# Attention and mixture-of-experts block: the eight attention heads that carry two chunks of expert weights moved from the 41st to 48th to the 49th to 56th

## What is computed

```python
h = _layernorm(x, axis=-1) * (1 + ca) + sa
x = x + ga * _L0_attn_ref(h, wq, wkv_a, wkv_b, wo)      # 16 heads, causal, latent k/v of 128, rope of 64
h = _layernorm(x, axis=-1) * (1 + cb) + sb
x = x + gb * _L0_ffn_ref(h, wa, rg, rgb, rw1, rb1, rw2, rb2, sg, sgb, sw1, sb1, sw2, sb2)
```

## Time and profile before

| | us |
|---|---|
| median of 3 runs | 1380.09 |
| the runs | 1380.09, 1387.56, 1379.63 |
| the profiled execution | 1384.28 |
| its span, first to last instruction | 1382.4 |

### The profile page before, as it was taken

One profiled execution on the slowest core, in us unless ns is written; L12 is line 12 of the kernel. 1 busy time (PEld: TensorE's weight loads), 2 busy tenths in 40 slices (PEclk: granted clock), 3 DMA queues, 4 the chain that ended last, 5 costly groups with the idle time before them and its releaser, 6 DMA issues. The chain is left out here.

```text
span 1382.4 us, 22778 instructions
## 1 busy us (share of the span) xinstructions
PE 1342.6 (97%) x6900; PEld 1113.9 (81%) x6900; DVE 854.7 (62%) x1753; ACT 672.2 (49%) x1551; POOL 385.0 (28%) x352
## 2 busy tenths in 40 slices
PE   6999999999999999999998999998999999999997
PEld 3667777888888888888887888887787888888885
DVE  5788745666666666666775666665766443434567
ACT  3334326666666666666665666664422332323222
POOL 0335465000012091030550120910023323223163
PEclk9999999999999999999999999999999999999999
DMA  9999989967677669696799866693827888887475
GB/s 293 369 345 373 367 299 310 338 216 226 202 275 265 227 227 321 200 336 203 241 362 330 303 204 231 219 362 128 324 101 273 304 323 333 314 333 265 129 226 171
DMA packets 160057, 375.57 MB, mean 272 GB/s; under 512 B 23164, under 2 KB 80576, under 8 KB 147696
## 3 DMA queue, kind: packets, MB, share of 16 engines
q1 hardware_dynamic: 144416, 314.32, 65.0%
q0 software_dynamic: 15568, 60.32, 12.4%
HBM read 245.84 MB, written 128.22 MB: 271 GB/s over the span
## 5 line engine op out<-in xcount | busy, mean ns | idle before, releaser
L1183 ACT ACTIVATE a_pr<-a_pr,a_stat 128x128 f32<-128x128 f32 (+3 forms) x256 | 142.3, 557 | 112.0 <-DVE a_stat L1258 111.7
L1258 DVE CUSTOM_DVE_ANT_0 a_pr<-a_psS,f_mask 128x128 f32<-128x128 f32 (+3 forms) x256 | 116.6, 486 | 33.1 <-PE a_psS L1366 30.7
L1189 ACT ACTIVATE a_pr<-a_pr,a_stat 128x128 f32<-128x128 f32 (+3 forms) x256 | 122.1, 549 | 0.5 <-DVE a_stat L1263 0.5
L1378 PE MATMUL a_psY<-a_pT,a_cv 128*128 128x512 f32 x564 | 120.5, 357 | 0.3 <-issue 0.3
L1378 PEld LDWEIGHTS a_psY<-a_pT,a_cv 128*128 128x128 f32 x564 | 101.4, 188 | 23.3 <-issue 0.7
L1202 ACT ACTIVATE a_pT<-a_psT 128x512 fp32r<-128x512 f32 x128 | 69.4, 597 | 79.0 <-PE a_psT L1394 79.0
L102 PE MATMUL a_psX<-a_hT,a_wqk 128*128 128x512 f32 (+1 forms) x256 | 101.3, 396 | 4.9 <-DVE a_pT L1286 4.3
L104 PE MATMUL a_psX<-a_hT,a_wqk 128*128 128x512 f32 (+1 forms) x256 | 101.6, 397 | 0.0
L103 PE MATMUL a_psX<-a_hT,a_wqk 128*128 128x512 f32 (+1 forms) x256 | 101.3, 396 | 0.0
L1274 DVE SCALAR_TENSOR_TENSOR a_qT<-a_psX,a_qT 128x512 fp32r<-128x512 f32 x64 | 44.3, 691 | 85.1 <-ACT a_qT L1193 85.1
L1286 DVE TENSOR_TENSOR a_pT<-a_psT,a_pT 128x512 fp32r<-128x512 f32 x128 | 82.1, 682 | 12.3 <-ACT a_pT L1202 12.3
(11 more groups left out here) (375 smaller groups left out, 3566.0 us busy)
## 6 DMA issues: line engine op xcount, KB each, us to landing
w1s_d<-a_ws SPq DMA_DIRECT2D x72, 512.0 KB, 3.6
a_wqk<-wqk_d SPq DMA_DIRECT2D x64, 512.0 KB, 4.6
a_mh<-mhl_d SPq DMA_DIRECT2D x32, 1024.0 KB, 5.9
s_ring<-w1s_d SPq DMA_DIRECT2D x16, 2048.0 KB, 9.3
w2s_d<-a_ws SPq DMA_DIRECT2D x72, 256.0 KB, 4.0
qpe_d<-p_qs SPq DMA_DIRECT2D x16, 1024.0 KB, 5.0
a_rw<-in_L_ffn_rw SPq DMA_DIRECT2D x128, 128.0 KB, 3.5
a_qpe<-qpe_d SPq DMA_DIRECT2D x64, 256.0 KB, 2.7
```

The costliest lines, as they stand in the source:

```text
L1183: nc.scalar.activation(pr[i], pr[i], ACT.Exp, bias=nmax[:, i:i + 1], scale=-1.0, accum_out=rsum[:, i:i + 1]).then_inc(ex, 1)
L1189: nc.scalar.activation(pr[i], pr[i], ACT.Copy, scale=rinv[:, i:i + 1]).then_inc(nr, 1)
L1258: nc.vector.tensor_tensor_reduce(out=pr[i], in0=score[i][:, 0:w], in1=mask[:, S - w:S], scale=-1.0, scalar=3e38, op0=ALU.add, op1=ALU.min, ...
L1378: last = nc.tensor.matmul(two_of(bank)[:, :, (2 - k) * P:2 * P], cv[:, j, cs], pT[:, :, ps, o:o + k * P], start=m == 0, stop=m == len(part ...
```

## The change

`DBL` goes from (10, 12) to (12, 14), so that the doubled heads are g = 48 to 55 and `EARLY` is 48. The phases move with it. In g = 40 to 47 the chunks of the routed experts come one a head, and the chunks of the shared experts are split eight heads later. The waits and the reads back of the shared experts' weights before the last group follow `EARLY`. The group left behind the doubled ones (m = 14) is written out in place of a loop over m = 12 to 14 on PE, ScalarE and SyncE, and over m = 14 alone on VectorE; VectorE gets a loop over m = 10 and 11. The groups m = 12 and 13 on VectorE now have both a second chunk and, in m = 13, the statistics of the norm.

```diff
--- before.py
+++ after.py
@@ -983,7 +983,7 @@
         ends = [psS[:, 2], psZ[:, :]]
         rest = [(B * PAIRS - 2, 3)] + [(B * PAIRS - 1, t) for t in range(TB)]
         two_of = lambda bank: bank.rearrange("p (u n) -> p u n", u=2)
-        DBL = (10, 12)
+        DBL = (12, 14)
         EARLY = DBL[0] * 4
 
         def run(eng, pair, norms=False):
@@ -1001,7 +1001,7 @@
                     two(m, 0)
                 for m in range(*DBL):
                     two(m, 1)
-                with eng.Fori(DBL[1], B * QB - 1) as m:
+                for m in range(DBL[1], B * QB - 1):
                     two(m, 2)
             else:
                 with eng.Fori(2, QB) as m:
@@ -1012,11 +1012,12 @@
                     two(m, 0)
                 two(2 * QB, 0)
                 two(2 * QB + 1, 0, 1)
-                for m in range(*DBL):
-                    two(m, 1)
-                two(3 * QB, 2)
-                two(3 * QB + 1, 2, 2)
-                with eng.Fori(3 * QB + 2, B * QB - 1) as m:
+                with eng.Fori(2 * QB + 2, DBL[0]) as m:
+                    two(m, 0)
+                assert DBL == (3 * QB, 3 * QB + 2)
+                two(DBL[0], 1)
+                two(DBL[0] + 1, 1, 2)
+                for m in range(DBL[1], B * QB - 1):
                     two(m, 2)
             pair(B * PAIRS - 2, 0, 4, False, 2, None)
             pair(B * PAIRS - 1, 1, 4, True, 2, None)
@@ -1103,7 +1104,7 @@
                 four(DBL[0] - 1, 4, 0)
                 for m in range(*DBL):
                     four(m, 4, 1)
-                with sp.Fori(DBL[1], B * H // 4 - 1) as m:
+                for m in range(DBL[1], B * H // 4 - 1):
                     four(m, 4, 2)
                 sp.wait_ge(ws_out[1], 32 * (EARLY // 2 + EXTRA + 1))
                 sp.dma_start(hT[:, 0].rearrange("p c s n -> p (c s n)").bitcast(F32),
```

## The result

| | before | changed |
|---|---|---|
| median of 20 runs each, us | 1380.95 | 1378.72 |
| lowest and highest | 1377.45, 1387.71 | 1375.42, 1382.33 |
| profiled execution, us | 1384.28 | 1378.67 |
| its span, us | 1382.4 | 1376.9 |

The ratio is 0.9973 with a 95% interval of 0.9962 to 0.9983: the kernel is 2.3 to 5.3 us faster. The prediction had 7.13 us, as a change of the median to 1373.0. The sign and the range of 1369 to 1381 held, the size did not.

What follows compares the result with a forecast made beforehand. TensorE, busy 97% of 1382.4 us, bounds the kernel, so only its idle or slow time can be gained. The stall's -7.13 us, all other terms 0, off the median 1380.09 gave 1372.96 us, range 1369 to 1381.

Steps and rivals of the forecast that it cites:

- The slack of 3.33 us: PE's spare time behind the late second chunk of g = 44: ScalarE waited 7.67 us, PE idled 4.34.
- the limit of 6.3 us between issue and landing: In doubled heads, a chunk landing more than 6.3 us after its issue costs PE time; a quiet pair needs 5.35 or less.
- nothing new would be lost: Eight chunks moved to g = 48 to 55 add no time on ScalarE, VectorE or DMA; at most 0.7 us if wrong.
- the 339 worked out for g = 48 and 49: GB/s of DMA traffic forecast for this first doubled pair: 7.87 MB in 23.2 us, including GpSimd's `a_cv`; cost 0.
- the 317: GB/s forecast for the three doubled pairs after g = 48 and 49, with no GpSimd transfer, like the pair at 750.
- The two terms put at 0 for the wait at g = 56 and for the loops: PE's wait of 0.42 us for `a_oT` at g = 56 stays; loops going or coming change nothing beyond 0.42 us.
- the bound of 0.42: Most that PE's wait at g = 56 could change, -0.42 to +0.42 us, also taken as the most for the loops.
- So the stall goes: -7.13 us: In heads 45 and 46, PE's 4.34 us of idle time and 2.79 of slow work disappear with single chunks.
- Rival 1: No gain, 1380.1 us: plain runs hardly have the stall, perhaps only the slowest and the profiled one; chance 0.17.
- Rivals 2 and 3: 2: small stall in g = 48 to 51, 1376 us, chance 0.09. 3: repeated stalls from g = 48, 1387.2 or 1394.4, 0.04.

## Why the prediction was right and wrong

- Where the stall is and whom it hits was right: the late chunk in `a_rw`, the slack of PE behind it, GpSimd's transfers as the cause. Moving GpSimd's 2 MB of loads alone left 0.61 us of it. The slack of 3.33 us, and the limit of 6.3 us between issue and landing built on it, hold only for a head's second chunk; behind a first chunk it is 1.1 to 1.3 us.
- That nothing new would be lost was right in every profile: g = 44 to 47, the doubled heads, and the heads with both a second chunk and the statistics. The pairs carry 290 and 332 GB/s for the 339 worked out for g = 48 and 49, and then 319 and 311 for the 317. Part of the first pair's traffic falls into the second.
- The two terms put at 0 for the wait at g = 56 and for the loops were not quite 0. The steps to g = 56 and 57, where VectorE's old loop began, are now 11.62 + 11.67 us for 12.07 + 11.79, 0.57 less and so beyond the bound of 0.42; those to g = 40 and 41, where its new loop begins, are 12.18 + 11.79 for 11.95 + 11.67, 0.35 more. The nine profiles with the old places and the ten with the new ones repeat each of these steps within 0.05 us. The prediction had looked for a cost of the loops at g = 48, where VectorE entered none. The second step of each pair goes with the loop: in every profile it is 11.75 to 11.80 us where VectorE enters a loop behind the statistics, at g = 24 too, and 11.64 to 11.68 where it enters none. At g = 8, where it enters one with no statistics ahead, the steps are the regular ones. The first step differs also where the loop does not, and how much of it is the loop's stays open. The two together, 0.22 us, are most of the rest of the 7.4 us by which attention differs between the two profiles.
- The step that failed is the term "So the stall goes: -7.13 us". The size was read from one execution and taken off the median of others, although that execution stood 4.19 us above this median. Over seven profiles the loss is 2.3 to 7.16 us with a mean of 5.2, and 5.0 +- 1.2 in plain runs; the execution profiled first was one of the two largest. Rival 1 had seen that the three runs lie 7.9 us apart, but read it as all or nothing. Its argument against, that the transfers are issued "at fixed places of the program, not at a margin", was false: in the same program `n_x` is issued from 0.11 us ahead of the chunk's last pieces to 3.5 us behind them, and the loss goes from 7.16 to 2.3 us.
- The second step that failed is one that the prediction does not have: it looked for what would be late next only in attention. About 2 us come back in the last stage, where PE's wait for expert weights is 0 to 3.1 us long, with up to 1.8 us of slow clock behind it. Why this costs the changed kernel more stays open. The stage's program is the same in both, and no profile showed what makes its chain of loads slower in one execution than in the next.
- Rivals 2 and 3 did not come true in the changed kernel. Rival 2 had 2 to 4 us of idle time for a small stall; where it was provoked, with 2.5 MB beside doubled heads, 1.65 us were lost. The forecast of 1372.96 stood 5.8 us below the measured median; that this lies inside 1369 to 1381 is owed to the width of the range, which reached up to rival 1.

## What to carry to other kernels

The stall from transfers of two queues meeting had a size of its own in each execution here. Profile a kernel two or three times before you take such a stall off a median, and look at the spread of its plain runs: here it was 10 us before and 7 after. Put a phase that refills its buffers on short terms where the other queue is silent, and when the gain of a stage doesn't arrive at the end, look for a later chain of loads that PE only just keeps ahead of. Leaving the later stage out of both kernels measured the first one's gain to +- 1.2 us with ten runs each.

## What the runs showed that was not expected

Which transfer is late, and by how much, went with the order in which SyncE and GpSimd issue: with `n_x` up to 0.11 us ahead, the second chunk is late by 7.5 us; with it 1.2 us or more behind, by at most 2.8. Waits of PE of much the same length cost differently: one of 1.91 us came with 1.7 us of missing clock and one of 1.89 with none, one of 2.1 us in the last stage with 1.8 and one of 2.5 with none. And loads in flight together paid: with the issue behind the landing one expert's 3 MB took 13.3 to 14.8 us, too slow for PE where an expert has two blocks; with the issue ahead of it they kept up with PE's 10.4.
